# Four chained cross-attention layers on one core: steps of the written order moved, and parts of layer 3's normalisations computed on GpSimd

## The reference

```python
q  = transpose(zt_prev + pos_enc); kv = transpose(za + pos_enc)      # 512 tokens of 256
q  = layer_norm(q, ln_q_g, ln_q_b);  kv = layer_norm(kv, ln_kv_g, ln_kv_b)
Q, K, V = split(q @ Wq), split(kv @ Wk), split(kv @ Wv)              # 16 heads of 16
ctx = softmax(Q K^T / 4) V
r = ctx @ Wo + q
h = layer_norm(r, ffn_ln_g, ffn_ln_b)
h = gelu(h @ W1 + b1) @ W2 + b2
out = transpose(h + r)
```

## Time and profile before

| | |
|---|---|
| median of 3 runs | 3172.9 us (3158.95 to 3174.35) |
| profiled execution, its own time | 3173.53 us |
| span of the profiled execution | 3171.7 us |
| PE busy | 2820.7 us, 89% |
| DVE busy | 1789.5 us, 56% |
| ACT busy | 1346.9 us, 42% |
| POOL busy | 881.6 us, 28% |
| mean granted TensorE clock | 0.942 of full |

### The profile page before, as it was taken

The page is one execution under the profiler, slowest core; times in us unless marked ns, Lnnn a source line. Parts: engine busy times, 40 slices in busy tenths (PEclk is TensorE's granted clock), DMA queues, the critical chain, the costliest instruction groups (busy, mean ns, idle before and its releaser), DMA issues.

```text
span 3171.7 us, 41543 instructions
## 1 busy us (share of the span) xinstructions
PE 2820.7 (89%) x14752; PEld 1335.6 (42%) x14752; DVE 1789.5 (56%) x4426; ACT 1346.9 (42%) x2373; POOL 881.6 (28%) x722
## 2 busy tenths in 40 slices
PE   6999998889999999989999999987868888888896
PEld 2322222235455555546556655643323333333333
DVE  4777777724443333312555675565677687567651
ACT  1666666643333333332344333422315544454563
POOL 1677777753344443310010001011111010101000
PEclk7999999999999999899999999998878999899998
DMA  5444444410002000112323333234233232323210
GB/s 116 101 106 108 103 103 103 119 56 28 25 28 85 28 28 21 68 54 74 69 57 70 65 69 73 54 71 90 64 102 87 58 88 49 84 65 75 55 47 26
DMA packets 182463, 219.94 MB, mean 69 GB/s; under 512 B 40968, under 2 KB 135792, under 8 KB 176112
## 3 DMA queue, kind: packets, MB, share of 16 engines
q1 hardware_dynamic: 170192, 189.74, 26.0%
q0 software_dynamic: 6016, 20.98, 1.9%
q10 hardware_dynamic: 6048, 6.56, 0.6%
HBM read 146.90 MB, written 51.64 MB: 63 GB/s over the span
## 4 chain that ended last, share of the span: by engine, by line
PE 56%; DVE 12%; DMA 10%; ACT 7%; SPq 6%; issue 5%; POOL 3%; ACTq 0%; DVEq 0%; POOLq 0%
PE PS L594 23%; PE PS L846 7%; DVE l_M L1491 3%; SPq L1735 3%; PE PS L983 3%; PE PS L963 2%; PE PS L973 2%; PE PS L765 2%; PE PS L915 2%; PE PS L1013 2%; PE PS L787 2%; PE PS L904 2%; PE PS L704 2%; PE PS L881 2%; PE PS L723 2%
## 5 line engine op out<-in xcount | busy, mean ns | idle before, releaser
L1491 DVE TENSOR_REDUCE l_M<-PS 128x1 f32<-128x512 f32 x512 | 334.7, 683 | 141.9 <-PE PS L963 139.3
L1270 DVE TENSOR_REDUCE l_M<-PS 128x1 f32<-128x512 f32 x512 | 331.4, 684 | 127.8 <-PE PS L704 127.6
L1208 ACT ACTIVATE l_P<-PS 128x512 f32<-128x512 f32 x512 | 286.3, 600 | 244.9 <-PE PS L973 228.2
L1574 POOL TENSOR_TENSOR l_S<-l_P 128x512 f32<-128x512 f32 x256 | 327.7, 1312 | 82.0 <-ACT l_P L1051 81.9
L1051 ACT ACTIVATE l_P<-PS 128x512 f32<-128x512 f32 x512 | 282.5, 597 | 111.8 <-PE PS L713 110.7
L1329 DVE TENSOR_REDUCE l1a_M<-PS 128x1 f32<-128x512 f32 x256 | 159.0, 684 | 246.6 <-PE PS L768 246.6
L963 PE MATMUL PS<-l_KS,l_QS 97*128 97x512 bf16 x512 | 205.6, 412 | 83.9 <-DVE l_M L1491 83.3
L1397 DVE CUSTOM_DVE_ANT_0 l_JK<-PS,l_MK 128x256 f32<-128x256 f32 x512 | 195.8, 420 | 136.9 <-PE PS L881 134.2
L973 PE MATMUL PS<-l_QS,l_KS 100*128 100x512 bf16 x512 | 206.3, 411 | 39.5 <-ACT l_P L1208 26.8
L704 PE MATMUL PS<-l_KS,l_QS 97*128 97x512 bf16 x512 | 205.4, 415 | 36.2 <-DVE l_M L1270 23.2
L846 PE MATMUL PS<-l_w_mlp_w,l_H 128*128 128x512 f32 x512 | 230.7, 598 | 5.9 <-ACT l1a_P L1104 5.0
(11 more groups left out here) (248 smaller groups left out, 4732.9 us busy)
## 6 DMA issues: line engine op xcount, KB each, us to landing
l_QS<-q_scratch SPq DMA_DIRECT2D x128, 128.0 KB, 5.6
q_scratch<-l_T SPq DMA_DIRECT2D x96, 128.0 KB
k_scratch<-l_T SPq DMA_DIRECT2D x96, 128.0 KB
l_QS<-q_scratch SPq DMA_DIRECT2D x32, 384.0 KB, 4.9
l_KS<-k_scratch SPq DMA_DIRECT2D x32, 384.0 KB
l_QS<-q_scratch SPq DMA_DIRECT2D x32, 256.0 KB, 5.5
l_KS<-k_scratch SPq DMA_DIRECT2D x32, 256.0 KB
l_RB<-l_recs SPq DMA_DIRECT2D x32, 256.0 KB
```

The source lines that it names most:

```text
L1208: e.activation(t.P[quad % 4][:, m, :], PS[:, COUNTS.bank[st], :], ACT.Exp, scale=0.25).then_inc(q.sem("act.exp", st), 1)
L1270: e.tensor_reduce(t.M[i % 2][:, qt, hd:hd + 1], PS[:, COUNTS.bank[st], :], AX.X, ALU.max).then_inc(q.sem("dve.smax", st), 1)
L1491: e.tensor_reduce(t.M[i % 2][:, qt, hd:hd + 1], PS[:, COUNTS.bank[st], :], AX.X, ALU.max).then_inc(q.sem("dve.smax", st), 1)
L1574: x = e.tensor_tensor(t.S[j % 2][:, m, :], t.P[2 * j % 4][:, m, :], t.P[(2 * j + 1) % 4][:, m, :], ALU.add)
```

## The change

Five things are changed. (1) In layer 3 three of the four instructions of `norm` (key scaling, gamma, beta) go from DVE to POOL; DVE keeps the first and signals POOL, and `tr` on PE waits for POOL. (2) `f2b` goes from DVE to POOL, and `f3` on PE waits for POOL. (3) The preparation of batches 1 to 7 starts at 2b - 0.1 in place of 2b - 0.95, so 0.85 beats later, with `tr` another 0.06 beats later. (4) In layer 2 the projection of the queries takes its bank from ring C. (5) Single steps of layers 0 to 2 are moved by 0.002 to 0.27 beats. The waits that follow from (1) and (2) are in the diff.

```diff
 # layer 0 and layer 1 (LATER likewise: 0.v on dve 0.05 -> 0.0367, 2.guess on dve 0.02 -> 0.022)
-        ... (0.3625, k("proj", 1)) ... (1.42, k("sq", 1)) ... (0.2, k("kproj", 1)) ... (0.45 + 0.12 * n, k("v", n))
+        ... (0.3492, k("proj", 1)) ... (1.4237, k("sq", 1)) ... (0.2406, k("kproj", 1)) ... (0.4956 + 0.12 * n, k("v", n))
 # layer 2
-            ... (0.04, k("yt", 1)) ... (0.9, k("gelu", 1)) ... (4.0 + (j + 0.5) * 0.034, k("smax", j)) ... (6.162, k("f1", 0))
+            ... (0.0646, k("yt", 1)) ... (1.1669, k("gelu", 1)) ... (4.0 + (j + 0.4279) * 0.034, k("smax", j)) ... (6.2449, k("f1", 0))
-  ... "2.qproj": ("A", "act.rest")
+  ... "2.qproj": ("C", "act.rest")
 # layer 3, order
-            at = -0.95 if b else 0.0
+            at = -0.1 if b else 0.0
-            out += [(at + 0.94, k("tr", 0)), (at + 0.97, k("tr", 1))]
+            out += [(at + 1.0, k("tr", 0)), (at + 1.03, k("tr", 1))]
 # PE, 3.tr and 3.f3
-                q.wait_ge("dve.norm", step("3.norm", 2 * b, 3))
+                q.wait_ge("pool.norm", step("3.norm", 2 * b, 3))
-                q.wait_ge("dve.f2b", step("3.f2b", i, 3))
+                q.wait_ge("pool.f2b", step("3.f2b", i, 3))
 # DVE
             if kind == "3.kst":
                 q.wait_ge("pool.kn", step("3.kn", 2 * b))
+                q.wait_ge("pool.norm", step("3.norm", 2 * b - 2, 3))
             elif kind == "3.norm":
-                x, k = t.QN[b % 4][:, j, :], t.KN[:, j, :]
+                x = t.QN[b % 4][:, j, :]
                 q.wait_ge("dve.newton", step("3.newton", 2 * b, 2))
-                q.next_needs(e.tensor_scalar(x, x, t.mv[:, j, 0:1], t.rs[:, j:j + 1], ALU.subtract, ALU.mult))
-                q.next_needs(e.tensor_tensor(x, x, t.gq[:, :], ALU.mult))
-                e.tensor_tensor(x, x, t.bq[:, :], ALU.add)
-                e.tensor_scalar(k, k, t.mv[:, 4 + j, 0:1], t.rs[:, 4 + j:5 + j], ALU.subtract, ALU.mult
+                e.tensor_scalar(x, x, t.mv[:, j, 0:1], t.rs[:, j:j + 1], ALU.subtract, ALU.mult
                                 ).then_inc(q.sem("dve.norm", st), 1)
             elif kind == "3.f1":
+                q.wait_ge("pool.f2b", step("3.f2b", i - 2, 3))
-            elif kind == "3.f2b":
...
 # POOL
+            elif kind == "3.norm":
+                x, k = t.QN[b % 4][:, j, :], t.KN[:, j, :]
+                q.wait_ge("dve.norm", st)
+                e.tensor_scalar(k, k, t.mv[:, 4 + j, 0:1], t.rs[:, 4 + j:5 + j], ALU.subtract, ALU.mult)
+                q.next_needs(e.tensor_tensor(x, x, t.gq[:, :], ALU.mult))
+                e.tensor_tensor(x, x, t.bq[:, :], ALU.add).then_inc(q.sem("pool.norm", st), 1)
+            elif kind == "3.f2b":
+                q.wait_ge("dve.newton", step("3.onewton", i, 2))
+                q.wait_ge("pe.tr", step("3.f3", i - 2, 3))
+                e.tensor_scalar(t.HH[:, j, :], t.QN[b % 4][:, j, :], t.mv2[:, j, 0:1], t.rs2[:, j:j + 1], ALU.subtract, ALU.mult
+                                ).then_inc(q.sem("pool.f2b", st), 1)
```

More of the change, by code:

```diff
@@ L25, in a1 @@
         k = lambda n, j=0: ("0." + n, b, h, j)
-        return [(0.0, k("proj", 0)), (0.1625, k("split", 0)), (0.3625, k("proj", 1)), (0.4125, k("split", 1)), (0.36 if (b, h) > (0, 0) else 0.52, k("stack", 0)), (0.6, k("stack", 1)), (0.61, k("mrow")),
+        return [(0.0, k("proj", 0)), (0.1625, k("split", 0)), (0.3492, k("proj", 1)), (0.4125, k("split", 1)), (0.36 if (b, h) > (0, 0) else 0.52, k("stack", 0)), (0.6, k("stack", 1)), (0.61, k("mrow")),
                 (0.6125, k("v", 0)), (0.8625, k("v", 1))]
@@ L67, in steps @@
             out += [(-0.3 if b else 0.0, k("lat", 0)), (-0.2 if b else 0.03, k("lat", 1))]
-        out += [(0.1, k("kproj", 0)), (0.2, k("kproj", 1)), (0.3, k("qproj", 0)), (0.37, k("qproj", 1))]
-        out += [(0.45 + 0.12 * n, k("v", n)) for n in range(4)]
+        out += [(0.1, k("kproj", 0)), (0.2406, k("kproj", 1)), (0.3, k("qproj", 0)), (0.37, k("qproj", 1))]
+        out += [(0.4956 + 0.12 * n, k("v", n)) for n in range(4)]
         out += [((1.05 + 0.2 * n) if (b, h) > (0, 0) else (1.46 + 0.1 * n), k("smax", n)) for n in range(4)] + [(1.8, k("rows")), (1.81, k("turn"))]
@@ L104, in steps @@
         if h == 0:
-            out += [(-0.6 if b else -2.0, k("yload")), (0.0, k("yt", 0)), (0.04, k("yt", 1))]
-            out += [(0.11 + 0.1 * j, k("fc1", j)) for j in range(8)] + [(0.8, k("gelu", 0)), (0.9, k("gelu", 1)), (0.9, k("lload"))]
+            out += [(-0.6 if b else -2.0, k("yload")), (0.0, k("yt", 0)), (0.0646, k("yt", 1))]
+            out += [(0.11 + 0.1 * j, k("fc1", j)) for j in range(8)] + [(0.8, k("gelu", 0)), (1.1669, k("gelu", 1)), (0.9, k("lload"))]
             out += [(1.16 + 0.1 * j + 0.126 * (j // 4), k("fc2", j)) for j in range(8)]
@@ L111, in steps @@
         out += [(3.513, k("qproj", 0)), (3.55, k("qsplit", 0)), (3.61, k("qproj", 1)), (3.63, k("qsplit", 1))]
-        out += [(4.0 + (j + 0.5) * 0.034, k("smax", j)) for j in range(16)] + [(4.57, k("rows")), (4.62, k("turn"))]
+        out += [(4.0 + (j + 0.4279) * 0.034, k("smax", j)) for j in range(16)] + [(4.57, k("rows")), (4.62, k("turn"))]
         for n in range(8):
@@ L121, in steps @@
         if h:
-            out += [(5.96, k("f0")), (6.162, k("f1", 0)), (6.24, k("f1", 1)), (6.66, k("guess"))]
+            out += [(5.96, k("f0")), (6.2449, k("f1", 0)), (6.24, k("f1", 1)), (6.66, k("guess"))]
             out += [(6.67 + 0.01 * n, k("newton", n)) for n in range(3)] + [(6.72, k("f3", 0)), (6.76, k("f3", 1))]
@@ L237 @@
     "2.f0": ["pool.f0"], "2.f1": ["pe.f1", "dve.f1", "dve.st"], "2.newton2": ["dve.newton"], "2.f3": ["dve.f3"],
-    "3.kn": ["pool.kn"], "3.qn": ["pe.lat", "dve.qn"], "3.newton2": ["dve.newton"], "3.norm": ["dve.norm"],
+    "3.kn": ["pool.kn"], "3.qn": ["pe.lat", "dve.qn"], "3.newton2": ["dve.newton"], "3.norm": ["dve.norm", "pool.norm"],
     "3.tr": ["pe.tr", "act.tr"],
@@ L243 @@
     "3.vals": ["pe.vals"], "3.out": ["act.vals"], "3.inv": ["dve.inv"], "3.f0": ["dve.f0", "pool.f0"], "3.f1": ["pe.f1", "dve.f1"],
-    "3.onewton2": ["dve.newton"], "3.f2b": ["dve.f2b"], "3.f3": ["pe.tr", "act.f3"], "3.f4": ["pe.f4", "act.f4"],
+    "3.onewton2": ["dve.newton"], "3.f2b": ["pool.f2b"], "3.f3": ["pe.tr", "act.f3"], "3.f4": ["pe.f4", "act.f4"],
     "3.gelu": ["act.gelu"], "3.f5": ["pe.f5", "dve.f5"],
@@ L1520, in vector3 @@
                     q.next_needs(x)
-            elif kind == "3.f2b":
-                q.wait_ge("dve.newton", step("3.onewton", i, 2))
-                q.wait_ge("pe.tr", step("3.f3", i - 2, 3))
-                e.tensor_scalar(t.HH[:, j, :], t.QN[b % 4][:, j, :], t.mv2[:, j, 0:1], t.rs2[:, j:j + 1], ALU.subtract, ALU.mult
-                                ).then_inc(q.sem("dve.f2b", st), 1)
             elif kind == "3.f5":
```

2 lines of the change are left out of this document (1 added, 1 removed), and 6 rows, old and new, of tables (FILLS, LATER).

## The result

The changed kernel takes 3114.75 us (median of 4 runs, 3111.67 to 3123.84), the kernel before beside it 3169.4 us (4 runs, 3158.95 to 3174.35). The ratio is 0.984, with a 95% interval of 0.980 to 0.987: 55 us less, where 33 were forecast. The profiled execution took 3112.9 us, with a span of 3111.1 and a mean granted clock of 0.949 (before: 3171.7 and 0.942).

A forecast was written before the change was run, and what follows sets the result against it. DVE was taken as the limit in layer 3's preparations, with PE idling. In us: 44.5 (old place) - 22.5 (new place) + 10 (batches 1, 2) - 1.8 (tail) + 3 (layer 2) = 33 off, 3140; range 3112 to 3170.

The forecast's parts named there:

- part 6: Layers 0 to 2: query projection in ring C 3 us off; other moves nothing, 5 off to 8 on.
- rival (c): Whole kernel smooths better than summed: no cost for bursts and ACT, full bank gain, better single steps; 3117, chance 0.09.
- Parts 1 and 2: Layer 3, batches 3 to 7: leaving the old place saves 8.9 us per batch, the new place costs 4.5.
- the bursts: Layer 3's new place: DVE work arriving in bursts costs 1.5 us per batch, bounds 0 to 6.9.
- the copies of `tr`: Layer 3's new place: four ACT copies queue behind the gelu, 1.3 us per batch, bounds 0 to 2.6.
- Part 3: Layer 3 on POOL: a `norm` step takes 2.2 us, `f2b` 3.2 per batch; hidden by cover, costing nothing.
- Part 4: Layer 3: POOL's work holds up DVE's `norm` instructions, 0 to 2.4 us per batch, 0.5 of it in the bursts.
- Part 5: Layer 3: batches 1 and 2 together 10 us off, batch 0 nothing; tail 1.8 us longer through `f2b` on POOL.
- The last sign under "What would show it": Layers 0 to 2 should end within some us of before; if not, part 6 is wrong.
- (a): Layer 3's new place turns as tight as the old; 10 us or less remain, 3163 to 3170, chance 0.18.
- (b): PE falls to its lower clock at layer 3's new place; 9 us slower per batch, 3205, chance 0.07.
- (d): Layer 3: nothing moves on the path, PE waiting for transfers or ACT anyway; 3153, chance 0.66 together with the forecast.

The follow-up runs named there:

- e3_l3_all: The kernel before with all changes of layer 3 alone, layers 0 to 2 and the ring as before; 3143.03 us, ratio 0.9914.
- e4_l3_place: The kernel before with layer 3's preparation (batches 1 to 7) at its new place, `tr` 0.06 beats later, `norm` and `f2b` on DVE; 3152.07 us, ratio 0.9939.
- e12_norm_only: The kernel before with three of four `norm` instructions on POOL, preparation at its old place, `f2b` on DVE; 3187.04 us, ratio 1.006.
- e8_last_dve: The changed kernel with `f2b` of the last batch back on DVE; 3112.93 us, ratio 0.9820 to the kernel before.
- e7_ring: The kernel before with only layer 2's query projection taking its bank from ring C in place of A; 3171.25 us, ratio 0.9999.
- e10_gelu: The kernel before with only layer 2's second gelu moved from beat 0.9 to 1.1669; 3161.68 us, ratio 0.9979.

## Why the prediction was right, and where it was not

**The sum was about right for layer 3 and far too small for layers 0 to 2.** 33 us were forecast, 55 measured, inside the range (3112 to 3170) but only 3 us above its lower end. That it lies inside is in part luck: layer 3 gave what was forecast of it, and the 22 us beyond the forecast came from layers 0 to 2, of which part 6 had 3 us in all. The time is nearest to rival (c), 3117, but not for its reasons: 14 of its 23 us more were to come from smoother bursts and ACT in layer 3, and layer 3 gave no more than the forecast.

**Parts 1 and 2 (old and new place), right, with a split that happened to fit.** By its terms the stretch from item 0 of layer 3 to `f1` 0 should lose the preparation of batch 3 and gain 6.4 us in batch 2, 15.3 us; it lost 21.7 (18.4 and 20.8 in e3_l3_all and e4_l3_place). From `f1` 0 to `f1` 5 there leave four at 8.9 us and arrive five at 4.5, 13.1 us; it was 9.2 in the changed kernel and 16.3 in e3_l3_all, whose code is the same there, so the 13.1 is neither confirmed nor refuted to better than some 4 us. To the end +1.8, measured +5.4. From item 0 of layer 3 on the terms give 26.6 us, the trace 25.5. That the place comes with fewer of the long periods of PE at a lower clock was in none of the terms. Of the single terms, the bursts (1.5 us) were about the 1.5 us wait for `qn` alone; the copies of `tr` (1.3 us) cost 3.1, but took away a wait of 3.7 that I had not set against them.

**Part 3 (POOL's prices), mis-sized.** 2.7 for 2.2 us and 4.9 for 3.2. The tensor_scalar that takes mean and scale from a tile is 1.22 us where half of the 128x512 one gave 0.75; the tensor_tensor, 0.73, was near the 0.65 taken. "It costs nothing, and 7 us of cover is what hides it" held for batches 3 to 7. It did not for batches 1 and 2, where PE waits 1.2 and 2.3 us for POOL. e12_norm_only shows the price at the old place, with 0.08 beats of cover in place of 0.14 and `f0` in the middle of `norm`: 17 us.

**Part 4 (in each other's way), right and too narrow.** 0.3 us in each of batches 3 to 7, and 1.8, 2.1 and 0.5 us in batches 0 to 2: within the bound of 0 to 2.4. Those of batches 0 and 1 came from POOL's work on layer 2, not from "POOL's work on the tile before", as part 4 had it. The largest holding of the kernel before lay in layer 1, 8.2 us on the path, where I had not looked.

**Part 5, right for batches 1 and 2 as far as the columns tell** (3.8 us lie in the column before). The tail was 3.4 for 1.8, by the price of part 3; e8_last_dve takes it back. The other 2.0 of the 5.4 us are PE's wait for POOL's `f2b` in front of `f3` of batch 6, which part 3 had at nothing.

**Part 6 failed.** "The other steps pass one or two neighbours. Together nothing" is the step. One of them, `v` of layer 1, passed one neighbour, and that was 12 us. Layer 2 gave 15 us for 3, and the 3 had the wrong owner: e7_ring gives nothing, e10_gelu 8 us, and the wait of the earlier trace rows goes with the gelu and not with the bank, which leaves 3.3 of its 4.6 us. I had bounded the moves (5 us off to 8 on) by how far they go, not by reading what stands at the place. The last sign under "What would show it" says as much: layers 0 to 2 ended 35 us earlier (some 5 of it before's own scatter), so part 6 is wrong.

**The rivals.** (a) is out: the period fell and PE's wait for maxima with it, from 47.0 us in 520 to 31.8 in as long a stretch of the changed kernel, less far than the 25 of "What would show it". (b) is out as a loss: the periods have clocks of 0.92 to 0.93, before 0.89 to 0.95, though a slow stretch does lie around the wait for ACT. (d), 3153, is out by the interval.

## What to carry to other kernels

A step's place and its engine are one decision: the same steps of two normalisations on POOL gave 9 us at one place and cost 24 at another (17 of them by `norm` alone), by what stood in the middle of them on POOL's list. Before a step's move is called small, look at the timelines of all engines where it lands: an instruction of 0.2 us that lies in front of PE's next work and beside a long one of POOL can be worth more than long ones off the path. And a wait that leaves a list may stand under another name: compare the sum of the waits, not the line.
